# Two 3x3 convolutions of a four-layer network: image rows held three times with four column tiles, against four strips with sixteen 32x32 tiles

## The reference, cut to what matters

```python
def _gn(v, G=16, eps=1e-5):        # group norm without weights, 2 channels a group
    ...
# x: (16, 32, 128, 128) float32
x = x + _L0_conv_ref(_gn(x), ...)
# layer 1 begins with   conv2d(input, offset_conv_w, offset_conv_b, padding=[(1,1),(1,1)])
x = x + _L1_conv_ref(_gn(x), ...)
# layer 2: lax.conv_general_dilated(x, weight, (1,1), ((1,1),(1,1)), NCHW) + bias
x = x + _L2_conv_ref(_gn(x), L2_conv_weight, L2_conv_bias)
x = x + _L3_conv_ref(_gn(x), ...)
```

## Time and profile before

| what | value |
|---|---|
| median of 3 runs | 21692.44 us (21674.75 to 21713.61) |
| the profiled execution's own time | 21728.42 us |
| its span, first to last instruction | 21726.9 us |
| mean granted TensorE clock | 0.897 |
| stage "l1o", first SyncE instruction to the start of the next stage's first | 6079.4 to 6879.7 us |
| stage "l2", the same | 16873.9 to 17758.6 us |

### The profile page before, as it was taken

One profiled execution on the slowest core, in us unless ns is written; L12 is line 12 of the kernel. 1 busy time (PEld: TensorE's weight loads), 2 busy tenths in 40 slices (PEclk: granted clock), 3 DMA queues, 4 the chain that ended last, 5 costly groups with the idle time before them and its releaser, 6 DMA issues. The chain is left out here.

```text
span 21726.9 us, 374304 instructions
## 1 busy us (share of the span) xinstructions
PE 16948.3 (78%) x128728; PEld 6960.4 (32%) x128728; DVE 14936.5 (69%) x15487; ACT 13323.2 (61%) x23402; POOL 10513.1 (48%) x6534
## 2 busy tenths in 40 slices
PE   6888888888833688888888759999996335667999
PEld 2333333333300222222222225555554002223444
DVE  8999999999921688888888735666666128883111
ACT  6899988898822566666666537878876223332111
POOL 5777877777700577777777620000003027772000
PEclk9999999999966899999999977988988667888999
DMA  2000000000098100000000041211213995552111
GB/s 72 12 12 12 12 12 12 12 12 12 25 167 154 44 18 19 18 18 18 19 18 18 21 84 24 39 33 33 39 33 92 181 207 108 111 108 57 43 44 41
DMA packets 1599601, 1091.44 MB, mean 50 GB/s; under 512 B 761144, under 2 KB 1452576, under 8 KB 1574056
## 3 DMA queue, kind: packets, MB, share of 16 engines
q1 hardware_dynamic: 1497624, 945.76, 21.1%
q0 software_dynamic: 26624, 100.67, 1.7%
q10 hardware_dynamic: 74448, 33.14, 0.6%
HBM read 863.66 MB, written 215.64 MB: 50 GB/s over the span
## 5 line engine op out<-in xcount | busy, mean ns | idle before, releaser
L323 DVE TENSOR_TENSOR l_mx<-l_p_v,l_puN 128x2048 f32<-128x2048 f32 x2560 | 5635.8, 2278 | 159.5 <-PE l_p_s L538 146.7
L538 PE MATMUL l_p_s<-l_mx,l_w2z 128*32 128x512 f32 x32768 | 3817.8, 610 | 585.7 <-ACT l_mx L450 314.8
L343 POOL TENSOR_TENSOR l_mx<-l_pv,l_puP 128x2048 f32<-128x2048 f32 x1024 | 3717.0, 3647 | 316.9 <-PE l_p_s L538 311.1
L1210 DVE TENSOR_TENSOR_SCAN l1m_hs<-l1m_da,l1m_carry,l1m_pu 128x512 f32<-128x512 f32 x2304 | 2823.3, 1267 | 106.1 <-ACT l1m_da L1126 2.2
L1868 ACT ACTIVATE l1d_ab<-l1d_pt 128x1024 f32<-128x1024 f32 x2304 | 2301.6, 1025 | 738.2 <-PE l1d_pt L1622 724.1
L1259 POOL TENSOR_TENSOR l1m_hc<-l1m_hs,l1m_cs 128x1024 f32<-128x1024 f32 x1152 | 2712.8, 2355 | 9.2 <-DVE l1m_hs L1210 5.7
L469 ACT ACTIVATE l_mx<-l_pv,l_puP 128x128 f32<-128x128 f32 x8192 | 2446.7, 393 | 0.8
L1746 DVE TENSOR_SCALAR l1d_hat<-l1d_ab 128x1024 f32<-128x1024 f32 x2304 | 1621.7, 704 | 825.8 <-ACT l1d_ab L1868 519.8
L1200 DVE TENSOR_TENSOR l1m_pu<-l1m_pu,l1m_bs 128x512 f32<-128x512 f32 x2304 | 1476.4, 687 | 751.8 <-PE l1m_pu L955 751.8
L450 ACT ACTIVATE l_mx<-l_mx 128x2048 f32<-128x2048 f32 x1024 | 1954.5, 1909 | 49.5 <-POOL l_mx L343 49.4
L1126 ACT ACTIVATE l1m_da<-l1m_pr,l1m_an 128x512 f32<-128x512 f32 x2304 | 1458.8, 684 | 824.6 <-PE l1m_pr L948 762.9
(11 more groups left out here) (326 smaller groups left out, 24908.7 us busy)
## 6 DMA issues: line engine op xcount, KB each, us to landing
n_xt<-x_after SPq DMA_DIRECT2D x48, 2048.0 KB
l3a_xs<-x_after SPq DMA_DIRECT2D x384, 256.0 KB, 5.3
l1o_img<-x_after SPq DMA_DIRECT2D x32, 2032.0 KB, 17.4
l_img<-x_after SPq DMA_DIRECT2D x32, 2032.0 KB, 17.3
l3a_xe<-x_after SPq DMA_DIRECT2D x480, 96.0 KB, 2.2
l1m_sq<-seq SPq DMA_DIRECT2D x256, 144.0 KB
n_xt<-in_x_dram SPq DMA_DIRECT2D x16, 2048.0 KB
l_xs<-in_x_dram SPq DMA_DIRECT2D x128, 256.0 KB, 2.9
```

The lines of the kernel that those rows point to most:

```text
L323: v.tensor_tensor(mx[:, r % QB, :, :, :], columns.unsqueeze(1).broadcast_to([P, 4, G, P]), rows.broadcast_to([P, 4, G, P]), ALU.max).then_ ...
L343: g.tensor_tensor(mx[:, r % QB, :, :, :], pv[:, u, :, :].unsqueeze(1).broadcast_to([P, 4, G, P]), rows.broadcast_to([P, 4, G, P]), ALU.add ...
L538: ins = pe.matmul(p_s[R * q:R * (q + 1), 512 * u:512 * (u + 1)], w2z[:, 31 - r:63 - r], mx[:, r % QB, q, :, :].rearrange("p t v -> p (t v) ...
L1210: dve.tensor_tensor_scan(hs[:, p % 3, part, :], da[:, p % 3, part, :], pu[:, LC * bank:LC * (bank + 1)], carry[:, u, c:c + 1], ALU.mult, A ...
```

## The change

`conv_layer` is written anew; nothing else but the layout of its weights changes.

- The image lies once in `img`: 32 channels by four strips of 32 rows, each strip with one row above and one below it (34 rows). Four DMAs load it. Only the border columns and border rows are cleared.
- The scales of all 16 images are loaded once, into all four groups of 32 partitions (four DMAs); VectorE copies those of one image into `gcur` (`choose`).
- ScalarE normalises 128 partitions: three pieces of a single row and one piece of 32 rows.
- TensorE uses sixteen 32x32 tiles: row tile g is the strip, column tile h is a block of four rows. Nine taps times 16 tiles for each of two halves of four banks, one bank a strip: 288 calls an image, and one small call at the head of each half.
- VectorE evacuates four banks when a half is done.
- Stores and, in "l2", residual loads are issued by ScalarE, in pieces of four rows (2 KB). SyncE issues image loads alone, each as soon as the convolution two images earlier has ended.

```diff
-        img = m.sb("img", [P, 2, H, WP])
+        img = m.sb("img", [P, 2, QR + 2, WP])
+        gn = m.sb("gn", [P, B, 2])
+        gcur = m.sb("gcur", [P, 2, 2])
+        def by_steps(t, b):
+            return t[at(b), :, :, :].rearrange("b c (q h i) w -> h (b c) q (i w)", h=4, i=RR)
...
+            def load(b, u):
+                for g in range(4):
+                    lo, hi = max(QR * g - 1, 0), min(QR * (g + 1) + 1, H)
+                    first = lo - (QR * g - 1)
+                    sp.dma_start(img[C * g:C * (g + 1), u, first:first + hi - lo, 1:W + 1],
+                                 x[at(b), :, lo:hi, :].rearrange("b c h w -> (b c) h w")).then_inc(img_in[u], 16)
...
             with sp.Fori(0, B // 2 - 1) as j:
                 for u in range(2):
-                    store(j * 2 + u, u)
+                    sp.wait_ge(conv_done, (j * 2 + u) * 2 + 2)
                     load(j * 2 + u + 2, u)
...
+                norm(slice(C, 2 * C), slice(0, 1))
+                norm(slice(2 * C, 4 * C), slice(0, 1))
+                norm(slice(0, 3 * C), slice(QR + 1, QR + 2))
+                norm(slice(0, P), slice(1, QR + 1)).then_inc(norm_done, 1)
+            def load_residual(b, u):
+                for h in range(4):
+                    act.dma_start(res[C * h:C * (h + 1), u], by_steps(x, b)[h]).then_inc(res_in[u], 16)
+            def store(b, u):
+                act.wait_ge(evac_done, b * NQ + 2 * NQ)
+                for h in range(4):
+                    act.dma_start(by_steps(out, b)[h], ot[C * h:C * h + keep, u]).then_inc(stored[u], 16)
+            normalise(0, 0, 1)
+            with act.Fori(0, B // 2 - 1) as j:
+                for u in range(2):
+                    normalise(j * 2 + (u + 1), 1 - u, j + (1 + u))
+                    store(j * 2 + u, u)
+                    if residual:
+                        load_residual(j * 2 + u + 2, u)
...
+                    for half in range(2):
+                        pe.wait_ge(evac_done, j * (2 * NQ) + (u * NQ + 4 * half + 4))
+                        pe.matmul(acc[0:C, 2048 * half:2048 * half + C], wt[:, 0, :], wt[:, 1, :], start=True, stop=True, tile_position=(0, 0))
+                        for tap in range(9):
+                            for h in range(4):
+                                r0 = 4 * RR * half + RR * h + tap // 3
+                                for g in range(4):
+                                    ins = pe.matmul(acc[C * h:C * (h + 1), 512 * (4 * half + g):512 * (4 * half + g + 1)], wt[C * g:C * (g + 1), tap, :],
+                                                    img[C * g:C * (g + 1), u, r0:r0 + RR, tap % 3:tap % 3 + W], start=tap == 0, stop=tap == 8,
+                                                    tile_position=(C * g, C * h))
                         ins.then_inc(conv_done, 1)
...
-            v.memset(img[:, 0, :, :], 0.0).then_inc(zeroed, 1)
-            v.memset(img[:, 1, :, :], 0.0).then_inc(zeroed, 1)
+            v.memset(img[:, :, :, 0:1], 0.0).then_inc(zeroed, 1)
+            v.memset(img[:, :, :, W + 1:W + 2], 0.0).then_inc(zeroed, 1)
+            v.memset(img[:, :, 0:1, 1:W + 1], 0.0).then_inc(zeroed, 1)
+            v.memset(img[:, :, QR + 1:QR + 2, 1:W + 1], 0.0).then_inc(zeroed, 1)
```

More of the change, by code:

```diff
@@ L580, in conv_layer @@
         block = ctx.enter_context(nc.Block())
+        N_LOAD = 9
+        def by_steps(t, b):
+            return t[at(b), :, :, :].rearrange("b c (q h i) w -> h (b c) q (i w)", h=4, i=RR)
         @block.sync
         def _(sp):
-            sp.dma_start(wt[:, :, :], weights).then_inc(w_in, 16)
+            sp.dma_start(wt[:], weights).then_inc(w_in, 16)
+            tb = table.rearrange("b (c q) s -> c b q s", c=C)
             for g in range(4):
                 sp.dma_start(bc[C * g:C * (g + 1), :], bias.rearrange("(p a) -> p a", a=1)).then_inc(w_in, 16)
-            sp.wait_ge(zeroed, 2)
+                sp.dma_start(gn[C * g:C * (g + 1), :, :], tb[:, :, 0, :]).then_inc(w_in, 16)
+            sp.wait_ge(zeroed, 4)
             def load(b, u):
[L590 to L607, removed]
+                for g in range(4):
[3 more added lines that the diff above has]
+                                 x[at(b), :, lo:hi, :].rearrange("b c h w -> (b c) h w")).then_inc(img_in[u], 16)
             load(0, 0)
@@ L617, in _ @@
             for u in range(2):
[L618 to L635, removed]
+                act.wait_ge(stored[u], (B // 2 + 1) * 64)
         @block.tensor
         def _(pe):
-            pe.wait_ge(w_in, 80)
+            pe.wait_ge(w_in, 16 * N_LOAD)
             with pe.Fori(0, B // 2) as j:
@@ L655, in _ @@
         def _(v):
-            v.memset(img[:, 0, :, :], 0.0).then_inc(zeroed, 1)
-            v.memset(img[:, 1, :, :], 0.0).then_inc(zeroed, 1)
[L659 to L663, removed]
-                for u in range(2):
[L665 to L676, removed]
@@ new lines, in _, with choose, drain @@
+            v.wait_ge(w_in, 16 * N_LOAD)
+            def choose(b, u):
+                v.tensor_scalar(gcur[:, u, :], gn[:, at(b), :].rearrange("p b s -> p (b s)"), 1.0, None, ALU.mult).then_inc(g_ready, 1)
+            def drain(b, u, pairs):
+                v.wait_ge(stored[u], pairs * 64 + 64)
+                if residual:
+                    v.wait_ge(res_in[u], pairs * 64 + 64)
+                for half in range(2):
+                    v.wait_ge(conv_done, b * 2 + (half + 1))
+                    for g in range(4):
+                        bank, q = acc[:, 512 * (4 * half + g):512 * (4 * half + g + 1)], 2 * g + half
+                        if residual:
+                            ins = v.scalar_tensor_tensor(out=ot[:, u, q], in0=bank, scalar=bc[:, 0:1], in1=res[:, u, q], op0=ALU.add, op1=ALU.add)
+                        else:
+                            ins = v.tensor_scalar(ot[:, u, q], bank, bc[:, 0:1], None, ALU.add)
+                        ins.then_inc(evac_done, 1)
@@ new lines, in _, with strip_conv @@
+            choose(0, 0)
+            choose(1, 1)
+            with v.Fori(0, B // 2 - 1) as j:
+                for u in range(2):
+                    drain(j * 2 + u, u, j)
+                    choose(j * 2 + (u + 2), u)
+            for u in range(2):
+                drain(B - 2 + u, u, B // 2 - 1)
+def strip_conv(w):
+    import numpy as np
+    o, i = w.shape[:2]
+    out = np.zeros((i, 9, T), np.float32)
+    out[:, :, :o] = w.reshape(o, i, 9).transpose(1, 2, 0)
+    return np.tile(out, (4, 1, 1))
```

41 lines of the change are left out of this document (25 added, 16 removed).

## The result

The changed kernel took **21082.4 us** (median of 4 runs, 21019.5 to 21104.6), the kernel before in the same session 21683.6 (4 runs, 21614.7 to 21713.6): ratio 0.9712, 95% interval [0.9688, 0.9737]. That is faster and inside the range of 20730 to 21120, but 220 us above the forecast of 20862 and nearer to rival 3 (21107) than to it. The profiled execution took 21070.2 us, its span is 21068.6.

The account below looks back on a forecast made before the run. Both stages were taken as bound by DMA with its many 512 B packets; savings of 434 us in "l1o" and 396 in "l2" took 21728.4 us to 20898, and 36.0 less for the median gave 20862 us, range 20730 to 21120.

Parts of the forecast that it names:

- rival 3: TensorE needs about 31 us an image, by less tile overlap, lower clock or fetching twice as slow; 21107 us; chance 0.13.
- TensorE's 17.5 us an image: Both stages: 15.4 us of matmuls against 17.0 of instruction fetching, taken as 17.5 with some of the loop's jump.
- 20.5 and 28 us of the periods: Time per image: 20.5 us in "l1o"; 28 in "l2", where DMA binds with a little dead time.
- stops of TensorE over 3 us a block: A sign in the profile after that would show the prediction wrong, a block being 256 fetched instructions.
- the upper bound of 34 us: TensorE's time an image if a fetched block costs a doubled 7.5 us beside full DMA queues.
- 18 rounds at 0.857 us: TensorE's work an image: 288 calls with all sixteen tiles running at once, 15.4 us.
- rival 4: Row tiles do not run beside column tiles: TensorE takes 61.7 us an image, slower at 22073 us; chance 0.04.
- a round of the buffers: Load, normalise and convolve in a buffer, shared by two buffers: 41.25/2 = 20.6 us an image in "l1o", 25.3 in "l2".
- Heads: Start of each stage: first matmul 26 us ("l1o") and 35 us ("l2") after SyncE's first instruction.
- 27.5 us an image: DMA time in "l2": 12.5 us of load plus 15.0 of residual and store, range 26.2 to 36.3.
- rival 2: 2 KB pieces are slow or hold up ScalarE: 36.3 us a period in "l2", 20987 us; chance 0.11.
- rival 5: The change does nothing for DMA, because a load's time goes by partitions and not packets; chance 0.02.

Follow-up runs that it names:

- after: The changed kernel with the whole change, against the kernel before: 21082.4 us, ratio 0.9712; loops 439.2 us in "l1o" and 529.9 in "l2".
- small_long: small with TensorE's loop again over two images, 2,320 instructions: loops 433.1 us in "l1o" and 546.7 in "l2".
- small: after with TensorE's loop over one image, images landing unpadded in their own buffer and normalised into one padded image: 20899.4 us, ratio 0.9621.
- taps8: after with eight of the nine taps, the last left out of the sum: loops 416.4 us in "l1o" and 487.0 in "l2".
- taps7: after with seven of the nine taps, the last two left out of the sum: loops 374.3 us in "l1o" and 461.6 in "l2".
- taps6: after with six of the nine taps, the last three left out of the sum: loops 298.1 us in "l1o" and 380.8 in "l2".
- small_pad: small with images landing in padded rows, in 512-byte pieces as in after: loops 338.0 us in "l1o" and 387.1 in "l2".
- small_res: small with the residual's loads issued by SyncE instead of ScalarE: loops 336.9 us in "l1o" and 352.1 in "l2"; timed again, 20758.9 us, ratio 0.9589.

## Why the prediction was right or wrong

**Right: what bound the kernel, and that DMA would be freed.** The image's load was the bound. SyncE issued the first image at 6074.60 and ScalarE began it at 6089.48, 14.9 us later (14.5 forecast); the DMA share in "l1o" is 0.56 of 27.4 us, 15.4 us an image (16.2 forecast). The scales alone gave next to nothing, 3.1 and 4.6 us.

**Wrong: TensorE's 17.5 us an image.** This is the step that failed, and with it the 20.5 and 28 us of the periods. Two things in it were off: how fetches and work go together, and the price of the work. That the time still lay in the range is owed to the width that rival 3 gave it, not to this step.

*The fetches.* The step counted them a little low (4.53 blocks an image, 5.4 measured) and priced a block at 3.75 us, from the earlier trace rows. It then took the larger of work and fetching, as if blocks arrived while matmuls ran. A block's matmuls take 128/288 x 9.75 = 4.3 us, more than 3.75, so by that no stop should be seen. But TensorE stood up to 4.5 us at a time; "stops of TensorE over 3 us a block" is what the prediction had named as its sign of being wrong. The 32 halves need 32 x 9.85 = 315 us with their dummies; the rest is 124 us in "l1o" and 215 in "l2". The waits of after account for most of it, here those of "l2" and then the jumps of "l1o":

```profile
PE l_acc L665 <- issue: 115.0, 40, 5.0
PE l_acc L660 <- DVE l_ot L694: 19.1, 7, 3.0
...
PE l1o_acc L660 <- DVE l1o_ot L696: 19.7, 7, 2.9
```

"l1o" has 63.4 us of stops and 19.7 at the jump, "l2" 115.0 and 19.1. The matmuls were also slower at the lower clock: busy 354.1 and 393.8 us where 315 are needed, 39 and 79 us. About a third of the loss is thus the clock and not the standing still. In all it is 7.7 and 13.4 us an image on top of the work. small_long against small prices the loop's length alone at 5.9 and 10.8 us an image. Work and fetching add up in part; the upper bound of 34 us in the prediction held this case, and rival 3 had a period near it, 31 us. Its mechanisms were others: the clock did not stay at the lower level (0.92 and 0.86), sixteen tiles did overlap, and that a fetch takes twice as long no run shows.

*The work.* 18 rounds at 0.857 us were taken, 18 at 1.083 were measured: 19.5 us instead of 15.4. Sixteen tiles do run at once, so rival 4 is refuted (it had 61.7 us an image), but a round of sixteen costs 0.23 us more than a round of four. The Trainium skill, page "TensorE: Matmul & The Clock Gate", section "Measured speedup vs the span model", was cited for 10.6 times. No run here has a single tile, so that figure is not tested; what these runs show is 4 x 0.857 / 1.083 = 3.2 times from four tiles to sixteen, where the step had 4, and 2.0 times from four to eight (0.857 and 0.84 us a round).

The sum by stage, the period being (loop - 22.5)/15, with 19.7 us for the last image's matmuls and 2.8 behind them: "l1o" 27.8 us instead of 20.5, 15 x 7.3 = 110 us less saved; "l2" 33.8 instead of 28, 87 us. Measured from SyncE's first instruction to the last evacuation, "l1o" saved 787.8 - 463.9 = 324 us (434 forecast), "l2" 872.0 - 572.2 = 300 us (396). The periods account for 197 of the 206 us that were missing, the head of "l2" for most of the rest. The two profiled executions differ by 34 us more than these stages do, which lies in stages that the change doesn't touch. The median missed by 220 us and not by 206 - 34 = 172, because the forecast put it 36 us under the profiled execution, where it lay 12 over it.

With the fetches gone (small) the same formula gives 21.0 and 23.4 us: in "l1o" nearly the 20.5 forecast, though by TensorE's 20.55 us of work and joint and not by a round of the buffers, and in "l2" the forecast of 28 was too high, by the DMA below.

**The room for a loop.** The prediction took a loop of 2,320 instructions as fetched each time, and that was right. One piece of its evidence was misread. Layer 0's loop has 624 matmuls a pass (39,936 over 64 passes), which the prediction took for some 630 calls. It is 1,248 loads and matmuls long, so its 6 fetches say nothing of a loop near 2,320.

Counted in loads and matmuls, the room ends between 1,552 and 1,808. The Trainium skill, page "Runtime: NRT & Kernel Launch", section "Instruction fetch mechanics", has a room of 2,048 instructions for TensorE, refilled in blocks of 256. As a limit for the loads and matmuls of a loop that is too high here. Counted in blocks fetched, the runs don't contradict it: after, taps8 and taps7 fetched 10.75, 9.75 and 8.75 blocks a pass, each 1.7 more than their loads and matmuls fill. With the same 1.7 blocks, an estimate, taps6 needs 7.8, under the page's 2048/256 = 8, and taps7 its 8.75, over them. Whether the 1.7 are waits and register instructions, blocks used in part at both ends of the loop, or fetching beyond its jump, no run shows.

**Heads.** "l1o": 24.5 us from SyncE's first instruction to the first matmul, 26 forecast. "l2": 42 instead of 35. Two images and two residuals, 8.6 MB, started together:

```profile
16513.68 6.19 ACTq L628 DMA_DIRECT2D l_res<-x_after  x8
...
16518.52 33.98 SPq L601 DMA_DIRECT2D l_img<-x_after  x8
...
16549.41 5.20 ACT L619 ACTIVATE l_img<-l_img,l_gcur 32x128 f32<-32x128 f32 x4 [86.37 <-DMA l_img<-x_after]
```

The first image landed 31 us after its issue; I had allowed 25.

**DMA in "l2"**: 27.5 us an image was too high. taps6, where TensorE has least to do, had 23.8 us an image at a share of 1.07, and small_pad 24.2. So the slow pieces of rival 2 (36.3 us) are refuted, and rival 5 with them; ScalarE held up by its queue, the other half of rival 2, was seen in small, for 21 us. The mistake was hidden, because TensorE needed more.

**ScalarE and VectorE**: 5.20 us an image (5.25 forecast) and 87.4/16 = 5.5 us an image for eight banks (6.0). That four DMA issues would hide under TensorE held in "l1o". In "l2" it held in after, whose TensorE left time for it, and no longer in small: there the residual's loads on ScalarE's queue cost 21 us, as small_res shows.

**Left open.** What one fetch costs when it isn't hidden. Why fetching is hidden over 635 matmuls in a row, five blocks (x87, x288 and x260), and not over the others; why "l2" pays twice as much for it (its DMA engines are busier, 0.79 against 0.56, but no run varied that alone); and what in a round of sixteen costs the 0.23 us. It isn't the order, and the calling alone doesn't explain it either: in the earlier trace rows 256 instructions ran in 1.89 us, so the 64 of a round would take 0.47 us, an estimate. That fetching can be hidden is seen in stage "l1d" of the kernel before: 406 blocks in 3853 us (12840 to 16693), 9.5 us each, with 16.9 us of stops named "issue" in all. In the two stages here a block is used up in 4.3 us.

## What to carry to other kernels

Splitting calls over more tiles multiplies instructions: count what a pass of TensorE's loop holds, and if the queue of instructions shows packets for every pass, shorten the body first, here by one image a pass, which shortened the two loops by 258 us, more than the 206 us that were missing. When fetching may not be hidden, price it on top of the work and not beside it. When one engine is freed, the next bound needs the more careful prices; here those were the fetches, taken as hidden, and TensorE's round, taken from a row with a quarter of the tiles.

## What the runs showed of the hardware that was not expected

- A loop of 1,552 loads and matmuls stayed resident, one of 1,808 was fetched anew on every pass (8.75 blocks of 16 KB), and the step between them was 76 us in 16 images, 35 of them the matmuls left out.
- Every loop that was fetched anew took 1.7 blocks a pass more than its loads and matmuls fill (taps7, taps8, after).
- Rounds over four, eight and sixteen tiles of 512 columns in float32 took 0.857, 0.84 and 1.083 us, the last in three orders of the sixteen.
- After a stop of 4.3 us the same half took 11.49 us at a granted clock of 0.83, instead of 9.75 us at 1.00; with the stops gone, the granted clock of the loop rose from 0.92 to 1.00 in "l1o" and from 0.86 to 0.98 in "l2" (small_res).
- Pieces of 17 KB in place of 512 bytes for the image gave nothing in "l1o" and 14 us of 387 in "l2".
